# Second half's queries spread over the first attention's steps instead of two blocks

## The reference, cut to what matters

```python
xn = _layernorm(x, ln_gamma, ln_beta)
q = (xn @ w_q).reshape(B, SQ, 16, 64)
k, v = jnp.split(context @ w_kv, 2, axis=-1)     # each reshaped to (B, SK, 16, 64)
scores = jnp.einsum("bqhd,bkhd->bhqk", q * 64 ** -0.5, k)
attn = jax.nn.softmax(scores, axis=-1)
out = jnp.einsum("bhqk,bkhd->bqhd", attn, v).reshape(B, SQ, 1024)
x = x + tanh(g) * tanh(gate) * (out @ w_out + b_out)
```

## Time and profile before

| | us |
|---|---|
| median of 3 runs | 306.22 (304.85, 306.22, 306.44) |
| the profiled execution, its own time | 306.4 |
| its span, first to last instruction | 304.7 |
| TensorE busy | 279.6 (92%) |
| VectorE, ScalarE, GpSimd busy | 192.5, 167.0, 96.0 |
| mean granted TensorE clock, share of full speed | 0.994 |

### The profile page before, as it was taken

How to read it: one execution, slowest core, us unless ns; L and a number is a source line. 1 busy time by engine, 2 the same in 40 slices (tenths; PEclk the granted TensorE clock), 3 DMA queues, 4 the chain that set the end, 5 groups by cost and what they waited for, 6 DMA issues and landing times.

```text
span 304.7 us, 6266 instructions
## 1 busy us (share of the span) xinstructions
PE 279.6 (92%) x2157; PEld 240.0 (79%) x2157; DVE 192.5 (63%) x607; ACT 167.0 (55%) x354; POOL 96.0 (32%) x144
## 2 busy tenths in 40 slices
PE   1999988789989989899999899999899999999995
PEld 0577865668878767788888699779689889999985
DVE  2798952688899997346767757655867722432106
ACT  2493346698886766423334564586716722556460
POOL 1167000666883443103006441010101540155510
PEclk9999999799999999999999999999999999999999
DMA  7799950000000000072000000000000145931122
GB/s 183 247 318 273 205 90 2 1 2 4 20 12 2 1 2 0 2 227 88 0 2 0 0 2 1 1 2 0 2 1 2 47 154 156 296 104 39 45 83 73
DMA packets 20526, 20.49 MB, mean 67 GB/s; under 512 B 2097, under 2 KB 15049, under 8 KB 20496
## 3 DMA queue, kind: packets, MB, share of 16 engines
q1 hardware_dynamic: 19088, 18.09, 22.1%
q0 software_dynamic: 1120, 1.88, 2.2%
q10 hardware_dynamic: 288, 0.13, 0.2%
HBM read 15.86 MB, written 4.24 MB: 66 GB/s over the span
## 4 chain that ended last, share of the span: by engine, by line
PE 65%; DVE 19%; POOL 5%; issue 4%; ACT 3%; DMA 2%; SPq 0%; DVEq 0%; ACTq 0%; POOLq 0%
PE bank L1251 10%; PE bank L1430 9%; PE bank L1224 7%; PE bank L1225 6%; PE bank L1226 6%; PE bank L1411 4%; PE bank L1418 4%; DVE xhat_sb L907 4%; PE bank L1209 4%; POOL p_sb L642 3%; DVE sum_sb L844 3%; PE bank L1169 2%; DMA ctx_tok_sb<-in_ctx 2%; PE bank L1180 2%; DVE negmax_sb L833 2%
## 5 line engine op out<-in xcount | busy, mean ns | idle before, releaser
L785 ACT ACTIVATE hT_sb<-bank,cols_sb 128x512 f32<-128x512 f32 x72 | 48.6, 689 | 52.9 <-PE bank L1226 52.4
L642 POOL TENSOR_TENSOR p_sb<-p_sb,recip_sb 128x480 f32<-128x480 f32 x32 | 31.6, 988 | 52.2 <-DVE recip_sb L847 52.2
L1146 DVE SCALAR_TENSOR_TENSOR x_sb<-bank,wts_sb,x_sb 128x128 f32<-128x128 f32 x96 | 27.0, 344 | 26.2 <-PE bank L1430 17.2
L1251 PEld LDWEIGHTS bank<-we_sb,hT_sb 128*128 128x128 f32 x320 | 37.1, 192 | 1.2 <-issue 0.5
L1251 PE MATMUL bank<-we_sb,hT_sb 128*128 128x128 f32 x320 | 38.0, 276 | 0.0
L694 POOL TENSOR_TENSOR rstd_sb<-veps_sb,minus_half_sb 128x4 f32<-128x4 f32 (+1 forms) x11 | 11.0, 998 | 66.8 <-DVE veps_sb L899 66.5
L1430 PE MATMUL bank<-w_sb,hT_sb 128*128 128x128 f32 x256 | 31.5, 276 | 0.0
L1430 PEld LDWEIGHTS bank<-w_sb,hT_sb 128*128 128x128 f32 x256 | 30.4, 192 | 1.2 <-issue 0.4
L1180 PE MATMUL bank<-ident_sb,p_sb 128*120 128x128 f32 x128 | 19.8, 280 | 7.7 <-POOL p_sb L642 7.4
L795 ACT ACTIVATE p_sb<-bank,bias_t_sb 128x128 f32<-128x128 f32 x60 | 17.0, 369 | 16.7 <-PE bank L1411 16.7
L1180 PEld LDWEIGHTS bank<-ident_sb,p_sb 128*120 128x120 f32 x128 | 13.6, 138 | 11.6 <-issue 10.1
(11 more groups left out here) (217 smaller groups left out, 610.1 us busy)
## 6 DMA issues: line engine op xcount, KB each, us to landing
xs_hbm<-col_rows_sb SPq DMA_DIRECT2D x1, 2145.0 KB, 17.5
we_sb<-in_L_ffn_We SPq DMA_DIRECT2D x1, 2048.0 KB, 8.8
w_sb<-in_L_ffn_We SPq DMA_DIRECT2D x8, 256.0 KB, 4.1
w_after_sb<-in_L_ffn_We SPq DMA_DIRECT2D x7, 256.0 KB, 3.4
w_kv_sb<-in_L_xattn_w_kv SPq DMA_DIRECT2D x2, 512.0 KB, 6.8
w_sb<-in_L_ffn_w SPq DMA_DIRECT2D x1, 1024.0 KB, 9.7
w_kv_sb<-xs_hbm SPq DMA_DIRECT2D x15, 65.0 KB, 3.1
x_sb<-in_x SPq DMA_DIRECT2D x1, 512.0 KB, 7.2
```

What stands on the lines that cost most here:

```text
L642: nc.gpsimd.tensor_tensor(p0[j % 4], p0[j % 4], recip0[:, j % 2, :].unsqueeze(2) .broadcast_to([128, HG, SK]), ALU.mult).then_inc(probs_re ...
L785: nc.scalar.activation(hT[:, u % 2, c, :], ps(item)[:, :], ACT.Relu if n == 1 else ACT.Silu, bias=cols[:, col:col + 1]).then_inc(read(item ...
L1146: last = nc.vector.scalar_tensor_tensor(out=x[:, b, :], in0=ps(key)[:, C * i:C * (i + 1)], scalar=w, in1=x[:, b, :], op0=ALU.mult, op1=ALU ...
L1251: last = nc.tensor.matmul(ps(key)[:, C * i:C * (i + 1)], hT[:, unit_at[(n, p, e)] % 2, c, 128 * i:128 * (i + 1)], we2[:, e, c, :], start=( ...
```

## The change

In the list, the eight items `("q0", c, 1)` stood in two blocks of four behind step 0 and step 1. Now one stands behind each of the steps 0 to 7, and the loop that emits steps with weight splits starts at 8, with the two splits of steps 4 and 6 written out behind that step's q0. So that the split query weights can live until step 7, they are allocated where `we2` lies, and given back before it; the load of `we2` therefore waits on SP for the last q0 matmul. Line numbers behind the first hunk of allocation move up by one.

```diff
-    late_queries = ((0, 1, 2, 3), (4, 5, 6, 7))
-    for i, chunks in enumerate(late_queries):
-        schedule.append(("attend", i))
-        schedule += [("q0", c, 1) for c in chunks]
+    for c in range(CH):
+        schedule += [("attend", c), ("q0", c, 1)]
+        if c >= 4 and c % 2 == 0:
+            schedule.append(("split", "w1", (c - 4) // 2))
...
-    for i in range(len(late_queries), STEPS + LY):
+    for i in range(CH, STEPS + LY):
...
         w2 = sb("w2", [128, E, HC0, C])
+        with ExitStack() as turn1:
+            def sb1(name, shape, dt=F32):
+                return turn1.enter_context(nc.sbuf_tensor(f"{name}_sb", shape, dt))
+
+            w_q_hi, w_q_lo = sb1("w_q_hi", [C, INNER], F32R), sb1("w_q_lo", [C, INNER], F32R)
         we2 = sb("we2", [128, E + 1, HC1, C])
...
-        with ExitStack() as turn1:
-            w_q_hi, w_q_lo = sb1("w_q_hi", [C, INNER], F32R), sb1("w_q_lo", [C, INNER], F32R)
         hot = sb("hot", [128, 2, B, E])
...
             load(w2[:], t["L0_ffn_w2"].rearrange("e (k p) c -> p e k c", p=128), "w2")
+            wait_full(sp, ("q0", CH - 1, 1))
             load(we2[:, 0:E], t["L1_ffn_We2"].rearrange("e (k p) c -> p e k c", p=128), "we2")
             load(we2[:, E], t["L1_ffn_Ws2"].rearrange("(k p) c -> p k c", p=128), "we2")
```

More of the change, by code:

```diff
@@ L356, in flamingo_kernel @@
         with ExitStack() as turn1:
-            def sb1(name, shape, dt=F32):
-                return turn1.enter_context(nc.sbuf_tensor(f"{name}_sb", shape, dt))
             ctxT_hi, ctxT_lo = sb1("ctxT_hi", [C, B * SK], F32R), sb1("ctxT_lo", [C, B * SK], F32R)
```

## The result

| | before | after |
|---|---|---|
| median of 4 runs, us | 305.97 (304.85 to 306.44) | 302.33 (301.93 to 302.48) |
| ratio, 95% interval | | 0.9881 (0.986 to 0.9902) |
| profiled execution, its own time / span | 306.4 / 304.7 | 301.93 / 300.2 |

The changed kernel is 1.2% faster, 3.6 us; the forecast was 301.9.

A forecast was written before the change was run, and what follows sets the result against it. Early attention was held by ACT's query-bank moves, lost overlap and a clock dip. A walk to s0(10,11) gained 4.3 us: 306.4 to 302.1, less 0.2 for the median, 301.9; own range 301.0 to 303.1, wider 300.0 to 304.3.

The forecast's parts named there:

- s0(2,3) and s0(4,5): Score pairs at the attention's start: s0(2,3) starts at 43.6 us in place of 50.07, s0(4,5) at 47.6.
- The loop: Steps 4 to 8: a round through scores, softmax, ACT's copy from bank 4 and q0 takes 5.76 us, gone round twice.
- s0(10,11): Score pair from which both orders are alike: starts at 62.5 us in place of 66.83, 4.3 us gained.
- The clock: Low clock at 57 to 60 us of before goes and no dip replaces it: 1.6 of the 4.3 us.
- A: Rival: the dip stays, 1.2 GHz for 3 us after the first pair or later; 303.9 us, chance 0.11.
- C: Rival: PE at 1.2 GHz through the spread steps, with short groups and waits; slower than before, 312 us, chance 0.03.
- The traffic: Late we2 and xs_clear loads, 4.4 MB beside the attention, cost 0 to 0.5 us; taken as nothing.
- Rival E: Traffic slows the attention's 26 us by more than a fifth, 5 us or more; over 306 us, chance 0.03.
- No giving back: Behind 66.83 us each engine's order is the same, so the gain is carried through to the end.
- B: Rival: loop slower than 5.76 us, by 0.8 a round, 1.6 in all; 303.9 to 304.9 us, chance 0.09.
- D: Rival: shorter waits on ACT, steps 4 to 8 at the steady 4.2 us; 298.8 us, chance 0.06.
- overlap: At the attention's start, some 9 us with only one score pair under way, softmax engines idle during the query items.

The follow-up runs named there:

- with bank 6: Changed kernel with the q0 items of steps 5 and 7 in bank 6, not bank 4 behind o0: 299.51 us, ratio 0.9804; repeated 300.21, 0.9806.
- the blocks with both helps: Kernel before, query blocks kept, with four banks for queries and unread matmuls on PE in the thin stretch: 301.72 us, ratio 0.986.
- The first experiment: Kernel before with its own query order, split query weights in we2's place, we2 and xs_clear loaded after the last q0 item: 306.1 us, ratio 1.0014.

## Why the prediction was right

- *s0(2,3) and s0(4,5)* (43.6, 47.6): 43.61 and 47.45. The last is 0.15 early: behind the transposes the q0 item costs 0.88 us from 46.57 to 47.45, and follows after 0.38 in place of 0.56.
- *The loop* (5.76 us a round): 5.88 and 5.87, through the chain it named, with PE waiting 1.07 and 1.08 us for the copy from bank 4 before the q0 items of steps 5 and 7. The term that was small is q0, 0.90 from 52.43 to 53.33 behind a wait in place of 0.80. Two of its terms were tested: without the split 0.30 less, without ACT's query move 0.40 less (predicted 0.50). Without the move ACT reaches the copy of o0 before PE has ended o0 (51.05 in that trace, the copy starts at 51.10), so 0.1 of it goes into waiting for PE.
- *s0(10,11)* (62.5, gain 4.3): 62.74, gain 4.08. The difference has three parts: 0.15 us early at s0(4,5), twice 0.12 late in the loop, and 3.54 us from s0(8,9) to s0(10,11) in place of the 3.4 of the walk.
- *The time* (301.9): 302.33. The walk's own bounds, 2.8 to 4.7, give 301.5 to 303.4 and not the 301.0 to 303.1 that the prediction put as its own range; the time lies in both.
- *The clock* (1.6 of the gain): shown. The clock line has no slice below the 9 after, all ten runs of the changed kernel had a mean clock of 0.998 or more, and filling PE's thin stretch in before gave 1.67 us in the trace, 1.25 in the median. The prediction took the one faster run of before, 1.4 and 1.6 us under the others, for the price of the dip; by the seven runs at full clock out of 45 that price is 0.8 to 1.3 us. Rivals A and C fall: in the kernel after PE goes through bank cycles with waits of 1.07 us at a granted clock of 1.00. The rule of the Trainium skill that spoke against the change (TensorE: Matmul & The Clock Gate, section A second HAM failure mode: psum-queue depth-cycling) is therefore not borne out by this kernel.
- *The traffic* (nothing): shown from both sides, 1.0014 with the loads added to before, and 21.81 against 21.80 us with the loads taken from after. Rival E falls.
- *No giving back*: 4.1 us at s0(10,11), at s0(26,27) and at the issue of `we1`. The profiled executions differ by 4.47; 0.4 of that comes after the attention, most of it in the second mixture, in work that the change doesn't touch: from SP's issue of the last expert inputs to that of the first expert results it takes 27.41 us in before, 27.10 in after and 27.32 in before with PE filled. The medians differ by 3.64, less than the 4.08 of the trace; why is left open.
- *B and D*: the rounds are neither over 6.5 nor at the steady 4.2 us. D fell for the reason given, the q0 item right behind o0 in one bank. Once that reason is removed the rounds take 4.73 and 5.00, most of the way to D: the whole kernel with bank 6 took 299.5 and 300.2, where D said 298.8. That is a different kernel, so it bears on D's reasoning and not on its forecast.

One reading was too kind. The prediction set "overlap" as the thing lost in before and 2.7 of the 4.3 us to its account. Lost were 2.24 us at the two query banks; four banks give them back with no overlap at all, and with the clock's 1.67 the blocks are level with the spread order. What the overlap adds on top is taken by the wait on bank 4, and only the version with bank 6 has it: 2.0 us in the trace and 2.4 in the medians on one chip. That these 2.0 us are overlap is a reading of two traces. From s0(0,1) to s0(10,11) PE is busy 18.89 of 19.78 us with bank 6, and in the blocks with both helps 20.65 of 21.97, of which 2.38 are matmuls that nobody reads.

Left open: how much of `we2`'s place itself matters. The spread order with the query weights in memory of their own and the loads early wasn't tried. The first experiment says only that the late loads are free.

## What to carry to other kernels

Before spreading a block of work between pipeline steps, look at which buffer each spread item will fill and who must read that buffer first: an item that stands right behind a producer in the same bank makes the whole engine wait for the reader, and with it all that is queued behind. Ask for each loss that an order seems to cause what its smallest remedy is (a further bank, work in a thin stretch); here two small ones together matched the reordering. A walk through one loop with durations from neighbouring rows, with the items behind a wait at the longer of their durations, was good to 0.1 us a round.

## What the runs showed of the hardware

- Work that nobody reads made the kernel faster: 8 matmuls of 512 columns, 2.4 us of PE, gained 1.25 us of 305.85 (0.9957, 0.9941 to 0.9974). In before a stretch with PE busy 1.00 of 3.00 us was followed by one at a clock of 0.50; with the matmuls it was busy 2.79 of 3.00, and full clock followed.
- The low clock is not a fixed property of the program: 5 of 23 runs of before on one chip, and 1 of 11 on each of two others, had a mean clock of 1.0.
- 4.4 MB at up to 312 GB/s beside the softmax left POOL's multiplication at 990 ns (988 without it) and DVE's sum at 642 (642); the whole kernel took 1.0014 times as long with the loads moved there (0.9996 to 1.0032).
